# Reciprocal rows by one narrow transpose and DMA, the mean subtracted in place, and a new order of the steps, in a four-layer graph network

## What is computed

```python
def layer0(h, adj, W, a):                    # graph attention
    Wh = h @ W.T
    e = leaky_relu((Wh @ a1)[:, :, None] + (Wh @ a2)[:, None, :], 0.2)
    return softmax(where(adj == 0, -inf, e)) @ Wh

def layer1(x, adj, W, a_1, a_2, a_12, W_1, W_2):
    h = x @ W
    z = leaky_relu(Ax + Ay + (h @ a_12) @ h.T, 0.2)
    return elu(x @ W_1 + softmax(where(adj > 0, z, -9e15)) @ x @ W_2)

def layer2(x, adj, ...):                     # four heads of 32 features
    s = q @ k.T / sqrt(32)                   # per head
    o = softmax(where(adj | eye, s, lowest)) @ v
    return relu(o @ Wo + bo)

def layer3(x, adj, ...):                     # relational graph convolution
    return relu(sum over relations r of (adj == r) @ ((x @ W + b_r) * sigmoid(g + bg_r)))  # here r = 1 alone

for layer in (layer0, layer1, layer2, layer3):
    x = layernorm(x + layer(x, ...))
```

## Time and profile before

| | |
|---|---|
| median of 3 runs | 498.07 us (496.0 to 498.63) |
| the profiled execution | 496.9 us, span 495.0 us (first to last instruction) |
| mean granted clock of TensorE | 0.988 of full speed |
| busy, share of the span | TensorE 95%, ScalarE 86%, VectorE 83%, GpSimd 75% |
| DMA queues, share of 16 engines | 18.4% for the kernel's own |

### The profile page before, as it was taken

The page is one execution under the profiler, slowest core; times in us unless marked ns, Lnnn a source line. Parts: engine busy times, 40 slices in busy tenths (PEclk is TensorE's granted clock), DMA queues, the critical chain, the costliest instruction groups (busy, mean ns, idle before and its releaser), DMA issues. The chain is left out here.

```text
span 495.0 us, 13988 instructions
## 1 busy us (share of the span) xinstructions
PE 468.4 (95%) x3872; PEld 402.3 (81%) x3872; DVE 410.8 (83%) x1605; ACT 428.0 (86%) x1261; POOL 370.6 (75%) x736
## 2 busy tenths in 40 slices
PE   6968999999999999999999999999999999999793
PEld 5756778988888888988888888888888888877572
DVE  5657898998888998898888988898898989876653
ACT  3558999999999999999999999999999999988750
POOL 1365576788888888888888888888888888986523
PEclk9989999999999999999999999999999999999997
DMA  7211111122112221222112221221123100000011
GB/s 219 74 44 44 44 54 52 40 63 66 40 48 66 66 66 54 54 66 63 36 56 66 65 60 51 66 65 43 45 66 87 34 23 13 23 24 23 22 45 44
DMA packets 40222, 26.93 MB, mean 54 GB/s; under 512 B 2641, under 2 KB 39889, under 8 KB 40146
## 3 DMA queue, kind: packets, MB, share of 16 engines
q1 hardware_dynamic: 40146, 26.03, 18.4%
HBM read 17.63 MB, written 8.39 MB: 53 GB/s over the span
## 5 line engine op out<-in xcount | busy, mean ns | idle before, releaser
L1211 POOL TENSOR_SCALAR x<-y,minus_mean,rstd 128x128 f32<-128x128 f32 x244 | 144.8, 601 | 6.8 <-issue 5.1
L788 ACT ACTIVATE p<-p,nmax 128x256 f32<-128x256 f32 x256 | 128.5, 530 | 0.4 <-DVE nmax L981 0.4
L981 DVE CUSTOM_DVE_ANT_0 p<-ps,neg 128x256 f32<-128x256 f32 x256 | 90.7, 420 | 2.3 <-PE ps L564 2.3
L1193 POOL TENSOR_TENSOR rstd<-ve,minus_half 128x2 f32<-128x2 f32 x128 | 91.1, 712 | 0.0
L575 PE MATMUL ps<-ident,p 128*128 128x128 f32 x512 | 78.0, 275 | 4.1 <-DVE nmax L981 3.4
L1186 POOL TENSOR_SCALAR ve<-stats 128x2 f32<-128x2 f32 x128 | 24.6, 192 | 72.3 <-DVE stats L896 64.9
L797 ACT COPY p2T<-ps 128x512 f32<-128x512 f32 x128 | 75.2, 590 | 1.3 <-PE ps L575 0.5
L575 PEld LDWEIGHTS ps<-ident,p 128*128 128x128 f32 x512 | 61.3, 143 | 9.3 <-DVE nmax L981 4.0
L788 ACT ACTIVATION_READ_ACCUMULATOR p<-p,nmax 128x1 f32 x256 | 56.1, 219 | 0.0
L896 DVE BATCH_NORM_STATS2 stats<-y 128x6 f32<-128x256 f32 x128 | 54.1, 423 | 1.5
L1175 POOL TENSOR_TENSOR relu<-relu,neg 128x512 f32<-128x512 f32 x32 | 37.1, 1161 | 21.1 <-ACT relu L757 21.1
(11 more groups left out here) (130 smaller groups left out, 1210.3 us busy)
## 6 DMA issues: line engine op xcount, KB each, us to landing
adj_in<-in_adj_dram SPq DMA_DIRECT2D x32, 256.0 KB, 3.0
xT<-in_xT_dram SPq DMA_DIRECT2D x32, 128.0 KB, 2.1
x_in<-in_x_dram SPq DMA_DIRECT2D x32, 128.0 KB, 2.1
x_aside<-x SPq DMA_DIRECT2D x32, 128.0 KB, 2.1
out_dram<-x SPq DMA_DIRECT2D x32, 128.0 KB, 2.9
l_w<-in_l_w_dram SPq DMA_DIRECT2D x1, 257.0 KB
l_w<-in_l_w_dram SPq DMA_DIRECT2D x1, 256.0 KB
first_w<-in_first_w_dram SPq DMA_DIRECT2D x1, 129.0 KB, 2.2
```

The lines of the kernel that those rows point to most:

```text
L788: last = nc.scalar.activation(p2(n)[:, k, a, :], p2(n)[:, k, a, :], ACT.Exp, bias=nmax2(n)[:, k, a:a + 1], scale=-1.0, accum_out=sum2(n)[: ...
L981: last = nc.vector.tensor_tensor_reduce(p2(n)[:, k, a, :], bank("sc2", n, a)[:, k * N:(k + 1) * N], neg2(n)[:, k, :], -1.0, HIGHEST, ALU.a ...
L1193: nc.gpsimd.tensor_tensor(rstd[layer](n), ve[layer](n), minus_half[:, :], ALU.pow)\
L1211: last = nc.gpsimd.tensor_scalar(dst[:, k, 0:D], y_t[layer](n)[:, k, :], minus_mean[layer](n)[:, k:k + 1], rstd[layer](n)[:, k:k + 1], ALU ...
```

## The change

`rs_rep` goes. `rs_rows` transposes the 128 x 8 reciprocals themselves, `c_rs` copies 8 rows of 128 out of PSUM, and a new step `rs_in` on SP spreads them by two DMAs inside SBUF, one for each tile of nodes: each of four rows is written to 32 partitions. `onT2` waits for these. The negated mean is no longer made; `norm` and `end_norm` subtract the mean that `moments` left. The order of the steps is new on all engines. In a round of TensorE it is now `proj0`, `sc2`, `pT1`, `v2`, `xT1`, `pT0`, `agg1`, `tT`, `agg0`, `pT2b1`, `agg3`, `xT3`, `pT2b0`, `agg2`, `s2_rows`, `z1`, `xw1`, `pT2a0`, `xT2`, `pT2a1`, `wo2`, `qk2`, `rs_rows`, `hg3`.

```diff
 PLAN = {
-    "sync": [("ld_xT", 6707), ("ld_adj", 7906), ("ld_w", 8043), ("ld_x", 8602), ("aside", 16291), ("store", 19013)],
-    "tensor": [("proj0", 8774), ("s2_rows", 9402), ("prep_a", 11038), ("pT0", 11053), ("prep_c", 11151),
-        ("agg0", 11161), ("prep_d", 11846), ("prep_b", 12046), ("xT1", 12143), ("tT", 12198), ("z1", 12448),
-        ("xw1", 12450), ("pT1", 12863), ("flag", 13095), ("agg1", 13150), ("xT2", 13535), ("qk2", 13667),
-        ("sc2", 13818), ("pT2b0", 14335), ("pT2a0", 14520), ("pT2a1", 14582), ("rs_rows", 15014), ("v2", 15091),
-        ("pT2b1", 15180), ("agg2", 15365), ("wo2", 15578), ("xT3", 16401), ("hg3", 16731), ("agg3", 17296)],
-    "scalar": [("c_proj0", 8986), ("c_s2", 9439), ("exp0", 10878), ("c_prep_a", 10907), ("c_pT0", 11066),
-        ("c_prep_c", 11302), ("c_prep_d", 11955), ("c_xT1", 12119), ("c_prep_b", 12238), ("c_tT", 12318),
-        ("relu1", 12513), ("c_xw1", 12553), ("exp1", 12734), ("c_pT1", 13058), ("c_elu1", 13159), ("c_xT2", 13557),
-        ("c_qk2", 13730), ("exp2b", 14126), ("exp2a", 14363), ("c_pT2b0", 14524), ("c_pT2a0", 14709),
-        ("c_pT2a1", 14722), ("c_rs", 15060), ("c_v2", 15069), ("c_pT2b1", 15262), ("c_xT3", 16468), ("gate3", 16807)],
-    "vector": [("masks", 9611), ("e0", 9640), ("m0", 10555), ("eq1", 10747), ("neg1", 10779), ("s0", 11213),
-        ("r0", 11373), ("y0", 11444), ("b0", 11520), ("flag_a", 11952), ("e1", 12743), ("r1", 13069), ("h1", 13108),
-        ("y1a", 13200), ("y1b", 13267), ("b1", 13417), ("flag_b", 13435), ("e2b", 14017), ("e2a", 14038),
-        ("r2", 14743), ("onT2", 15553), ("y2a", 15795), ("y2b", 15854), ("b2", 15915), ("end_norm2", 16376),
-        ("vals3", 16995), ("y3", 17485), ("b3", 17599), ("end_norm3", 18642)],
-    "gpsimd": [("var0", 11545), ("rsq0", 11592), ("norm0", 12023), ("neg2", 12065), ("rmask1", 12520),
-        ("var1", 13324), ("rsq1", 13342), ("norm1", 13471), ("rs_rep", 14753), ("var2", 16029), ("rsq2", 16104),
-        ("norm2", 16213), ("var3", 18121), ("rsq3", 18145), ("norm3", 18673)],
+    "sync": [("ld_xT", 6817), ("ld_adj", 6943), ("ld_w", 7141), ("ld_x", 8627), ("rs_in", 14745), ("aside", 18557),
+        ("store", 19861)],
+    "tensor": [("proj0", 8944), ("s2_rows", 9359), ("prep_a", 10462), ("pT0", 11102), ("agg0", 11198),
+        ("prep_c", 11353), ("prep_b", 11938), ("prep_d", 12067), ("xT1", 12099), ("tT", 12171), ("z1", 12415),
+        ("xw1", 12437), ("pT1", 13072), ("agg1", 13140), ("xT2", 13473), ("qk2", 13719), ("sc2", 14038),
+        ("flag", 14148), ("pT2b0", 14338), ("pT2a0", 14456), ("pT2a1", 14528), ("rs_rows", 14850), ("v2", 15078),
+        ("pT2b1", 15269), ("agg2", 15343), ("wo2", 15634), ("xT3", 16296), ("hg3", 16875), ("agg3", 17272)],
+    "scalar": [("c_proj0", 9032), ("c_s2", 9429), ("exp0", 10902), ("c_pT0", 11202), ("c_prep_a", 11393),
+        ("c_prep_c", 11619), ("c_prep_d", 11932), ("c_xT1", 12123), ("c_tT", 12347), ("c_prep_b", 12414),
+        ("relu1", 12466), ("c_xw1", 12643), ("exp1", 12776), ("c_pT1", 13056), ("c_elu1", 13322), ("c_xT2", 13721),
+        ("c_qk2", 13762), ("exp2b", 14231), ("exp2a", 14383), ("c_pT2b0", 14506), ("c_pT2a0", 14724),
+        ("c_pT2a1", 14760), ("c_rs", 14810), ("c_v2", 15072), ("c_pT2b1", 15330), ("c_xT3", 16386), ("gate3", 16847)],
+    "vector": [("e0", 9654), ("masks", 9827), ("neg1", 9873), ("m0", 10595), ("eq1", 10972), ("s0", 11255),
+        ("r0", 11284), ("y0", 11305), ("b0", 11547), ("flag_a", 11979), ("e1", 12725), ("r1", 13144), ("h1", 13218),
+        ("y1a", 13236), ("y1b", 13266), ("b1", 13286), ("e2b", 14127), ("e2a", 14132), ("flag_b", 14538),
+        ("r2", 14653), ("onT2", 15622), ("y2a", 15770), ("y2b", 15905), ("b2", 16019), ("end_norm2", 16295),
+        ("vals3", 17068), ("y3", 17330), ("b3", 17390), ("end_norm3", 18434)],
+    "gpsimd": [("neg2", 10099), ("var0", 11629), ("rsq0", 11759), ("norm0", 11973), ("rmask1", 12606),
+        ("var1", 13266), ("rsq1", 13428), ("norm1", 13515), ("var2", 16026), ("rsq2", 16098), ("norm2", 16244),
+        ("var3", 17679), ("rsq3", 18208), ("norm3", 18743)],
 }
...
         stats = [ring(f"stats{k}", [T, 3], of="small") for k in range(4)]
         ve = [ring(f"ve{k}", [T], of="small") for k in range(4)]
-        minus_mean = [ring(f"minus_mean{k}", [T], of="small") for k in range(4)]
         rstd = [ring(f"rstd{k}", [T], of="small") for k in range(4)]
...
         sum2 = ring("sum2", [T, HEADS], of="small")
         rsum2 = ring("rsum2", [T, HEADS])
-        rs_rep = ring("rs_rep", [T, D], of="rs_row")
+        rs_turned = ring("rs_turned", [P], of="rs_row")
...
                     sp.dma_start(dst, src).then_inc(sem("weights_loaded"), 16)
+            def rs_in(n):
+                sp.wait_ge(sem("rs_sb"), n + 1)
+                free(sp, "rs_row", n, "onT_sb")
+                for k in range(T):
+                    sp.dma_start(rs_row(n)[:, k * P:(k + 1) * P],
+                                 rs_turned(n)[k * HEADS:(k + 1) * HEADS].rearrange("h (a i) -> h a i", a=1)
+                                 .broadcast_to((HEADS, DK, P))).then_inc(sem(f"rs_in{n % RING['rs_row']}"), 16)
+
             def aside(n):
...
             sp.dma_start(first_w[:, :], t["first_w"]).then_inc(sem("w0_loaded"), 16)
-            run("sync", {"ld_adj": ld_adj, "ld_xT": ld_xT, "ld_x": ld_x, "ld_w": ld_w, "aside": aside, "store": store})
+            run("sync", {"ld_adj": ld_adj, "ld_xT": ld_xT, "ld_x": ld_x, "ld_w": ld_w, "rs_in": rs_in, "aside": aside, "store": store})
             for s in range(RING["x4"]):
...
                 o = bank("rs_rows", n)
                 bank_free(pe, "rs_rows", n)
-                pe.wait_ge(sem("rs_rep_ready"), n + 1)
-                for k in range(T):
-                    last = pe.transpose(o[:, k * P:(k + 1) * P], rs_rep(n)[:, k, :], ident[:, :])
-                last.then_inc(sem("rs_ps"), 1)
+                pe.wait_ge(sem("rsum2_ready"), n + 1)
+                pe.transpose(o[0:T * HEADS, 0:P], rsum2(n).rearrange("p t h -> p (t h)"), ident[:, :])\
+                    .then_inc(sem("rs_ps"), 1)
...
             def c_rs(n):
                 act.wait_ge(sem("rs_ps"), n + 1)
-                free(act, "rs_row", n, "onT_sb")
-                nc.scalar.copy(rs_row(n), bank("rs_rows", n)[:, 0:N]).then_inc(sem("rs_sb"), 1)
+                if n >= RING["rs_row"]:
+                    act.wait_ge(sem(f"rs_in{n % RING['rs_row']}"), 16 * T * (n // RING["rs_row"]))
+                rows = slice(0, T * HEADS)
+                nc.scalar.copy(rs_turned(n)[rows, :], bank("rs_rows", n)[rows, 0:P]).then_inc(sem("rs_sb"), 1)
...
                 dve.wait_ge(sem("p_ready2a"), n + 1)
                 dve.wait_ge(sem("p_ready2b"), n + 1)
-                free(dve, "rsum2", n, "rs_rep_ready")
+                free(dve, "rsum2", n, "rs_ps")
                 nc.vector.reciprocal(rsum2(n), sum2(n)).then_inc(sem("rsum2_ready"), 1)
...
             def onT2(n):
                 dve.wait_ge(sem("agg_ps2"), n * HEADS + HEADS)
-                dve.wait_ge(sem("rs_sb"), n + 1)
+                dve.wait_ge(sem(f"rs_in{n % RING['rs_row']}"), 16 * T * (n // RING["rs_row"] + 1))
                 free(dve, "onT", n, "wo_ps")
...
             def end_norm(layer, n):
-                dve.wait_ge(sem(f"mean{layer}_ready"), n + 1)
+                dve.wait_ge(sem(f"stats{layer}_ready"), n + 1)
                 dve.wait_ge(sem(f"rstd{layer}_ready"), n + 1)
...
                 for k in range(T):
                     last = nc.vector.tensor_scalar(dst[:, k, 0:D], y_t[layer](n)[:, k, :],
-                                                   minus_mean[layer](n)[:, k:k + 1], rstd[layer](n)[:, k:k + 1],
-                                                   ALU.add, ALU.mult)
+                                                   stats[layer](n)[:, k, 1:2], rstd[layer](n)[:, k:k + 1],
+                                                   ALU.subtract, ALU.mult)
                 last.then_inc(sem(f"x{layer + 1}_ready"), 1)
...
                 nc.gpsimd.tensor_tensor(relu(n), relu(n), neg1(n), ALU.add).then_inc(sem("rmask_ready"), 1)
-            def rs_rep_(n):
-                pool.wait_ge(sem("rsum2_ready"), n + 1)
-                free(pool, "rs_row", n, "rs_ps")
-                nc.gpsimd.tensor_copy(rs_rep(n).rearrange("p t (h d) -> p (t h) d", h=HEADS),
-                                      rsum2(n).rearrange("p t (h a) -> p (t h) a", a=1)
-                                      .to_broadcast([P, T * HEADS, DK])).then_inc(sem("rs_rep_ready"), 1)
-
             def variance(layer, n):
...
                 nc.gpsimd.tensor_scalar(ve[layer](n), stats[layer](n)[:, :, 2], 1.0 / D, EPS, ALU.mult, ALU.add)\
                     .then_inc(sem(f"ve{layer}_ready"), 1)
-                nc.gpsimd.tensor_scalar(minus_mean[layer](n), stats[layer](n)[:, :, 1], -1.0, None, ALU.mult)\
-                    .then_inc(sem(f"mean{layer}_ready"), 1)
...
             def norm(layer, n):
```

(7 more changed lines are left out.)

## The result

The changed kernel took 523.93 us (median of 4 runs, 522.02 to 524.91) against 497.03 us before on the same chip: 1.0538 times as long, with an interval of 1.0485 to 1.0591. The forecast was 493.9. All times and ratios here are of fast runs; a single run, of d3, fell into the slow state (603.35 us at a granted clock of 0.751) and is left out. The profile of the changed kernel has a span of 521.7 us, 26.7 more than before. By the starts of `proj0`, 2.2 us of that are lost before the ninth graph's (79.48, before 77.30), 15.4 from there to the last graph's (416.99, before 399.39) and 9.1 behind it. What changed there is shown one by one.

What follows compares the result with a forecast made beforehand. TensorE's own work was taken to bound the dense middle, latency chains fill and drain. Gains of 3.3 + 0.45 + 0.4 = 4.2 us off the median 498.07 gave 493.9 us; range 491 to 499.

Steps and rivals of the forecast that it cites:

- The step that failed first: Norm on GpSimd: subtracting the mean has the same shape as the addition before, so it was counted as nothing.
- The second: GpSimd's five steps from var2 to norm2, ahead of xT3: about half a microsecond to spare, counted as nothing.
- The new order takes it back: Rival: norm2 over half a microsecond late makes xT3 wait each round; 0.11 us cancels the middle's gain, 497.2 us; chance 0.17.
- the gain of 0.11 a round: TensorE, rs_rows: one narrow transpose instead of two shrinks the slot from 0.22 to 0.11 us.
- The third: Landing of each rows transfer inside SBUF: taken as 2.1 us, 4.0 at the far end; counted as hidden.
- The rival on the drain: Fill and drain: weights ahead of ld_xT cost 1.5 us, late last rows make onT2 wait 1.5; 496.9 us; chance 0.12.
- Queued behind the waiting SP: Loads of xT and adj and the store, behind the rows transfers: lose about one microsecond of twenty-eight, counted as nothing.
- Start: Fill, with loads, preparation steps and masks reordered: taken as even, 0, between -1.5 and +1.5 us.
- the first rival: The narrow transpose drains TensorE: slot 0.27 to 0.44 us, 3.9 us lost less 0.85 gained, 501.1 us; chance 0.13.
- The round of 13.89 us: Sign that the forecast is right: TensorE's round in the middle is 13.89 us, from 14.00 before.
- where 3.3 had been reckoned: TensorE, one transpose fewer: 0.11 us in each of 30 rounds, 3.3 us gained.
- The two terms for GpSimd's copies: Copies dropped on GpSimd: 0.45 us gained in the last graph's norm chain, 0.4 in fill and drain waits for x.

Runs made afterwards that it cites:

- d3: c8 with the variance of layer 0 alone moved ahead of the mask of layer 1's relu on GpSimd: 495.4 us, 0.9969 of the kernel before.
- c3: The kernel before, with GpSimd's copy holding the mean itself and the norm subtracting that copy: 525.36 us, 1.0571.
- c4: The kernel before, with the norm adding the mean from the statistics, so only its time is of use: 496.28 us, 0.9989.
- c1: The changed kernel with the negated mean put back, copied by GpSimd and added in the norm: 505.3 us, 1.0174 of the kernel before.
- c8: c1 with the reciprocals written four times side by side, so each transfer reads 16 partitions instead of 4: 501.68 us, 1.0082 of the kernel before.
- e1: The changed kernel, subtraction kept, with the variances of layers 0 and 3 ahead of the mask and transfers reading 16 partitions: 497.86 us, 1.0006.
- d4: The changed kernel, subtraction kept, with the variances of layers 0 and 3 ahead of layer 1's mask on GpSimd: 504.32 us, 1.0149.
- e3: c1 with the rows as before, GpSimd's copy of the reciprocals ahead of the mask, so only the order is new: 502.58 us, 1.0100.
- d2: The kernel before with the rows part alone, transfers reading 16 partitions, order and norm untouched: 492.27 us, 0.9906.
- e2: The kernel before, in its own order, with the subtraction and the rows by transfers reading 16 partitions: 494.46 us, 0.9952.
- d1: The kernel before with the rows part alone, transfers reading 4 partitions, order and norm untouched: 553.53 us, 1.1136.

## Why the prediction was wrong

**The step that failed first** is this one: "The subtraction of the mean in the norm has the shape of the addition before: nothing." Shape was taken for price. The trace of before had no subtraction on GpSimd, so the operation was an unknown that should have been bounded from both sides, like the narrow transpose. It measured 0.27 us more an instruction (c3 against c4), 244 times.

**The second** let it through: "From `var2` at 205.33, 2.03 into the round, that is 6.2: about half a microsecond to spare. I count nothing." The five steps (4.2 with gaps) took 4.0 in c1 and 4.6 with the dear norm. Their start was taken from the old order as a fixed place in the round, 2.03 behind `proj0`. In both orders it hangs on what stands ahead: GpSimd gets to `var2` through `norm3` and `norm0` from the mask that waits for `z1`, a loop of one round, which no sum of a single stretch shows. The new order puts a second variance into that path and takes room out of it at `xT3`: `var2` began 2.67 into the round in c1 and 2.86 in the changed kernel. `xT1`, which closes the loop first (c1, 14.07), was not looked at. The rival "The new order takes it back" had the right mechanism (`xT3` waiting for `norm2`) and priced it by where it cancels the gain of 0.11 a round; the wait went on to 0.87.

**The third** is a size: "Each is bounded by these, and I take 2.1", with 4.0 as the far end. The second transfer landed 6.83 us after its issue, at a DMA share of 0.17; from 16 partitions it was 2.4 (c8). The rival on the drain foresaw a late landing with a wait of 1.5 us; it was 3.9 on VectorE and 3.8 on TensorE, and at the fallen clock the matmuls behind it took nearly twice as long. By c8 against c1 and e1 against d4 this is worth 3.6 to 6.5 us. "Queued behind the waiting SP ... they lose about one microsecond" was 2.4 for each issue; in the middle that cost nothing, since c8 and c1 have the same round.

**Start**: "0, between -1.5 and +1.5" was too kind. Graph 1's `proj0` began at 8.33 instead of 6.54, and the order alone lost 3 us before the dense stage (e3).

**What held.** The narrow transpose has a slot of 0.11 us, and its weights are loaded at 224.17, 0.22 ahead of its matmul, so TensorE isn't drained: the first rival falls. The Trainium skill (TensorEngine Tiling (Array Packing), Restrictions and Gotchas) says that column tiling and the transpose mode of FP32 exclude each other; the slot agrees with a transpose that is not tiled. The round of 13.89 us stands in d2, d3, d4, e1 and e2 as forecast, and d2 alone yields 4.1 us, against 4.2 in the sum. The gain was there, in the old order and with other transfers. That the two totals agree is in part luck: d2 keeps the negated means, whose going was to give 0.45, and by its profile the fill gave 0.5 us and the stretch from the ninth `proj0` to the last 2.6, where 3.3 had been reckoned. The two terms for GpSimd's copies were not measured by themselves.

The loss can be taken apart along two paths. From 523.9: the mean put back, 18.6; 16 partitions, 3.6; one variance moved, 6.2; the old order, 3.2; that is 492.3. Or: two variances moved, 19.6; 16 partitions, 6.5; that is 497.9. (The kernel before lay between 496.3 and 498.2 beside these runs, so a term is good to a microsecond or two.)

## What to carry to other kernels

When an instruction keeps its shape but changes its operation, its price is unknown: bound it or measure it alone. In a new order, follow the path of each engine from an operand through its queue and back to the same step one round later; such a loop can set the round while no engine is full, and then the place of two steps, 0.33 us together, was worth 19.6 us here. Look at the slowest dimension of a transfer (4 landed in 6.8 us here, 16 in 2.4), and at the DMA share while it runs alone.

## What the runs showed of the hardware

- On GpSimd a tensor-scalar instruction of 128x128 with subtract and multiply takes 0.79 us at best and 0.87 to 0.96 on average (c3, d4, e2), with add and multiply 0.44 to 0.45 and 0.49 to 0.60 (d1, c4); an operand in a tile of three words a row costs no more than a compact one (601 ns in c4 and before, 871 in d4 and c3). VectorE took the same for both operations, 3.6 us for twelve.
- Of two transfers of 64 KB inside SBUF from 4 partitions each, the second landed 6.8 us after its issue, and the two issues behind them on SP were held for 2.4 us each; from 16 partitions it is 2.4 us, and 0.4 to 0.6.
- After an idle time of 3.77 us in the drain TensorE's granted clock was 0.50 for the last 15 us, and eight matmuls took 2.05 us for 1.13.
- A transpose with weights of 8 or of 32 columns has a slot of 0.11 us on TensorE, the same as one of 128 (the changed kernel, d2, before).
